# Three steps of each gate's second half summed by TensorE alone, nine reductions there shortened by a second GpSimd addition

## What is computed

```python
def _gate(h, q, Wg, bg, Wq, bq):            # q: 8 x 64 x 768, h: 256 x 768
    h3 = h.reshape(B, N, F)                  # B = 8 blocks of N = 32 nodes
    hg = einsum('bnf,gf->bng', h3, Wg[:, :F])
    qg = einsum('blf,gf->blg', q, Wg[:, F:]) + bg
    attn = sigmoid(hg[:, :, None, :] + qg[:, None, :, :])
    qi = einsum('bnlf,blf->bnf', attn, q)    # sum over the 64 query rows l
    alpha = sigmoid(h3 @ Wq[:, :F].T + qi @ Wq[:, F:].T + bq)
    return alpha * tanh(qi) + (1 - alpha) * h3
```

## Time and profile before

| | us |
|---|---|
| median of 3 runs | 823.54 (823.35 to 824.70) |
| the profiled execution's own time | 824.55 |
| its span in the trace | 822.7 |
| PE busy | 774.9 (94%) |
| DVE busy | 603.2 (73%) |
| POOL busy | 514.3 (63%) |
| ACT busy | 423.7 (52%) |

### The profile page before, as it was taken

How to read it: one execution, slowest core, us unless ns; L and a number is a source line. 1 busy time by engine, 2 the same in 40 slices (tenths; PEclk the granted TensorE clock), 3 DMA queues, 4 the chain that set the end, 5 groups by cost and what they waited for, 6 DMA issues and landing times.

```text
span 822.7 us, 10528 instructions
## 1 busy us (share of the span) xinstructions
PE 774.9 (94%) x4176; PEld 639.7 (78%) x4180; DVE 603.2 (73%) x660; ACT 423.7 (52%) x505; POOL 514.3 (63%) x219
## 2 busy tenths in 40 slices
PE   7999999999988999988898889999999999998998
PEld 4669986776645699667665558999999999975886
DVE  8966239999999631888999997764696498565462
ACT  6424447677664342766676725434442454253731
POOL 0625609999998273599999955770785177805500
PEclk9999999999999999999999999999999999999999
DMA  9037525345332463360153327556356446250001
GB/s 364 31 81 232 170 81 154 89 142 154 115 116 77 137 231 131 77 179 2 52 205 116 115 78 282 180 193 227 116 163 216 159 154 209 99 230 0 2 1 39
DMA packets 24409, 111.01 MB, mean 135 GB/s; under 512 B 3620, under 2 KB 6180, under 8 KB 23976
## 3 DMA queue, kind: packets, MB, share of 16 engines
q1 hardware_dynamic: 23240, 104.24, 39.2%
q10 hardware_dynamic: 1120, 6.10, 1.9%
HBM read 100.63 MB, written 0.79 MB: 123 GB/s over the span
## 4 chain that ended last, share of the span: by engine, by line
PE 57%; POOL 19%; DVE 18%; ACT 3%; issue 2%; DMA 0%; DVEq 0%; ACTq 0%
PE ps L1076 27%; POOL prod L582 13%; DVE prod L1958 10%; PE ps L1107 5%; PE ps L1042 5%; POOL prod L585 4%; DVE qi_t L1976 3%; PE ps L1589 3%; PE ps L1234 2%; PE ps L1255 2%; POOL w_lo L570 2%; PE ps L1413 1%; PE ps L1650 1%; PE ps L1235 1%; PE ps L1304 1%
## 5 line engine op out<-in xcount | busy, mean ns | idle before, releaser
L570 POOL TENSOR_TENSOR w_lo<-w_raw,w_hi 128x1536 fp32r<-128x1536 f32 x49 | 183.9, 3764 | 141.6 <-ACT w_hi L662 141.5
L582 POOL TENSOR_TENSOR prod<-prod 128x1024 f32<-128x1024 f32 x94 | 222.8, 2392 | 46.0 <-DVE prod L1958 45.8
L798 ACT ACTIVATE prod<-ps 128x1024 f32<-128x1024 f32 x192 | 187.3, 1023 | 73.3 <-PE ps L1366 61.0
L1958 DVE TENSOR_TENSOR prod<-prod,ps 128x2048 f32<-128x2048 f32 x96 | 217.8, 2281 | 5.1 <-ACT prod L798 3.4
L662 ACT ACTIVATE w_hi<-w_raw 128x1536 fp32r<-128x1536 f32 x60 | 88.9, 1487 | 119.6 <-PE ps L1076 108.2
L1366 PE MATMUL ps<-sel_pair,h_and_q 128*128 128x512 f32 x384 | 128.4, 447 | 16.8 <-ACT prod L798 16.5
L1076 PE MATMUL ps<-w_hi,yt_hi 128*128 128x384 f32 x480 | 123.0, 337 | 0.2 <-POOL w_lo L570 0.2
L1076 PE MATMUL ps<-w_hi,yt_lo 128*128 128x384 f32 x480 | 122.0, 335 | 0.0
L1076 PE MATMUL ps<-w_lo,yt_hi 128*128 128x384 f32 x480 | 122.0, 335 | 0.0
L1366 PEld LDWEIGHTS ps<-sel_pair,h_and_q 128*128 128x128 f32 x384 | 67.0, 190 | 52.0 <-ACT prod L798 31.8
L1042 PE MATMUL ps<-w_raw,h_t 128*128 128x384 f32 x312 | 106.8, 486 | 0.0
(11 more groups left out here) (247 smaller groups left out, 1093.1 us busy)
## 6 DMA issues: line engine op xcount, KB each, us to landing
w_raw<-weights SPq DMA_DIRECT2D x105, 768.0 KB, 4.4
wa_in<-weights SPq DMA_DIRECT2D x6, 768.0 KB, 5.9
w_gat<-weights SPq DMA_DIRECT2D x6, 768.0 KB, 8.0
w_query<-weights SPq DMA_DIRECT2D x3, 768.0 KB, 11.7
h_and_q<-stage_hi SPq DMA_DIRECT2D x24, 96.0 KB, 2.1
h_and_q<-stage_lo SPq DMA_DIRECT2D x24, 96.0 KB, 2.2
a_vec<-gat_vectors ACTq DMA_DIRECT2D x1, 2048.0 KB, 9.7
q_t<-queries ACTq DMA_DIRECT2D x1, 1536.0 KB, 10.5
```

Of the source, the lines that this page charges most:

```text
L570: pool.tensor_tensor(Wl[:, j, :], raw_slab(U, 0, j), Wh[:, j, :], ALU.subtract).then_inc(w_lo_by_pool, 1)
L582: pool.tensor_tensor(v[:, :, 0:32], v[:, :, 0:32], v[:, :, 32:64], ALU.add).then_inc(folded_once, 1)
L798: act.activation(slot_view(s)[:, :, 32 * u:32 * u + 32], args.rearrange("p b (n l) -> p (b n) l", l=LH), ACT.Sigmoid).then_inc(sigmoid_rea ...
L1958: TT(slot_view(s), slot_view(s), ps[:, 6, o:o + L].unsqueeze(1).broadcast_to([P, NB, L]), ALU.mult).then_inc(products_ready, 1)
```

## The change

In each gate's second half three steps that were "tensor" become "whole": 32, 41 and 43 in gate 0, and 32, 35 and 38 in gate 1. POOL does nothing for a "whole" step, and PE folds all 2048 columns with sixteen identity products instead of eight; both pieces of the sigmoid of step s + 4 then wait for this fold. Nine steps that were "vector" become "pool": 34, 37, 40, 42 and 45 in gate 0, and 34, 40, 42 and 44 in gate 1. Places in the order do not move.

```diff
-ALONE = [(4, 10, 16, 25, 27, 28, 30, 34, 37, 40, 42, 45), (25, 27, 28, 30, 34, 40, 42, 44)]
+ALONE = [(4, 10, 16, 25, 27, 28, 30), (25, 27, 28, 30)]
+WHOLE = [(32, 41, 43), (32, 35, 38)]
 def kind_of(i, s):
+    if s in WHOLE[i]:
+        return "whole"
     if s + 3 in FOLD_AT[i]:
         return "tensor"
     return "vector" if s in ALONE[i] else "pool"
...
+        def by_tensor(i, s):
+            return count_kind(i, s, "tensor") + count_kind(i, s, "whole")
+        def by_pool(i, s):
+            return (STEPS - 1) * i + s + 1 - count_kind(i, s, "whole")
...
             def fold(i, s):
+                if KIND[i][s] == "whole":
+                    return
...
                     if s >= PSLOTS:
-                        if u == 1:
-                            act.wait_ge(folded_once, (STEPS - 1) * i + (s - PSLOTS + 1))
-                        elif KIND[i][s - PSLOTS] == "tensor":
-                            act.wait_ge(fold_ready, count_kind(i, s - PSLOTS, "tensor"))
+                        if u == 1 and KIND[i][s - PSLOTS] != "whole":
+                            act.wait_ge(folded_once, by_pool(i, s - PSLOTS))
+                        elif KIND[i][s - PSLOTS] in ("tensor", "whole"):
+                            act.wait_ge(fold_ready, by_tensor(i, s - PSLOTS))
...
                     bank7_free(at_)
-                    pe.wait_ge(folded_once, (STEPS - 1) * i + (s + 1))
+                    n = 8
+                    if KIND[i][s] == "whole":
+                        pe.wait_ge(products_ready, STEPS * i + (s + 1))
+                        n = 16
+                    else:
+                        pe.wait_ge(folded_once, by_pool(i, s))
...
-                    for k in range(8):
-                        mm = pe.matmul(o, ident[:], slot_view(s)[:, :, 4 * k:4 * k + 4], start=(k == 0), stop=(k == 7))
+                    for k in range(n):
+                        mm = pe.matmul(o, ident[:], slot_view(s)[:, :, 4 * k:4 * k + 4], start=(k == 0), stop=(k == n - 1))
```

More of the change, by code:

```diff
@@ L79 @@
 KIND = [[kind_of(i, s) for s in range(STEPS - 1)] for i in range(2)]
-REST_AT = [[s + (3 if KIND[i][s] == "tensor" and KIND[i][s + 1] != "tensor" else 2) for s in range(STEPS - 1)] for i in range(2)]
+REST_AT = [[s + (3 if s + 3 in FOLD_AT[i] and s + 4 not in FOLD_AT[i] else 2) for s in range(STEPS - 1)] for i in range(2)]
 QUERY_EVENTS = [0, 1, 5, 6]
@@ L583, in fold @@
                 if KIND[i][s] == "pool":
-                    pool.wait_ge(folded_once, (STEPS - 1) * i + (s + 1))
+                    pool.wait_ge(folded_once, by_pool(i, s))
                     pool.tensor_tensor(v[:, :, 0:16], v[:, :, 0:16], v[:, :, 16:32], ALU.add).then_inc(folded_twice, 1)
@@ L1966, in reduce @@
                         terms = slot_view(s)
-                    elif KIND[i][s] == "tensor":
-                        dve.wait_ge(fold_ready, count_kind(i, s, "tensor"))
+                    elif KIND[i][s] in ("tensor", "whole"):
+                        dve.wait_ge(fold_ready, by_tensor(i, s))
                         terms = ps[:, 7, 0:4 * NB].rearrange("p (n l) -> p n l", l=4)
@@ L1973, in reduce @@
                     else:
-                        dve.wait_ge(folded_once, (STEPS - 1) * i + (s + 1))
+                        dve.wait_ge(folded_once, by_pool(i, s))
                         terms = slot_view(s)[:, :, 0:32]
```

## The result

| | us |
|---|---|
| median of the changed kernel, 4 runs | 829.74 (829.16 to 830.85) |
| median of the kernel before, 4 runs | 823.88 (823.35 to 824.70) |
| ratio | 1.0070, 95% interval 1.0055 to 1.0084 |
| span of the profiled execution (before) | 827.4 (822.7) |
| DVE busy (before) | 599.3 (603.2) |

The change makes the kernel slower by 5.9 us (0.7%), with less work on both engines that bound the gates. The forecast was 827.7, so 2.0 us too low; the measured time lies just inside the upper end of its range (829.8). Of the 2.0 us, 0.3 is the median before, which was 823.54 over three runs and is 823.88 over four; 1.7 is the change itself, forecast at +4.2.

A forecast was written before the change was run, and what follows sets the result against it. DVE and POOL were taken to share the bound in the gates' second halves, with the order of waits deciding. Gate 0 +2.4 and gate 1 +1.8 gave +4.2 us, from 823.54 to 827.7; range 825.2 to 829.8 for 8 in 10.

The forecast's parts named there:

- The direction and the mechanism: Both gates' second halves: slower because POOL's chain decides, 827.7 us, own range 826.3 to 829.2; chance 0.78.
- Gate 0, +2.4: Gate 0's second half: POOL's additions delay reduction 40 and product 43; +2.4 us, bounds +1.9 to +3.6.
- step 32 gives nothing: Gate 0: the dropped addition's 2.33 us give nothing, since step 33 waits for DVE's product anyway.
- step 40's first addition: Gate 0, POOL: it starts at 248.36 instead of 245.75, after second additions of 1.25 and 1.36 us.
- the shift shrinks by one shortened reduction: Gate 0, DVE after product 43: the shift falls from +2.97 to +2.45 us, 0.52 less.
- Gate 1, +1.8: Gate 1's second half: the last reduction ends at 487.8 instead of 486.02; +1.8 us, bounds +0.7 to +2.8.
- The lead of dropped additions 35 and 38: Gate 1, POOL: starts step 39 at 457.5 instead of 459.47, a 2.0 us lead, all it keeps of three dropped additions.
- PE's long folds cost nothing: PE: folds of sixteen products, taken as 3.56 us, cost nothing yet but have no slack at gate 0's end.
- PE becomes the bound: Rival: sixteen products hold PE 4 us or more, gate 0 ends at +3.4, gate 1 hides it; 828.7 us; chance 0.08.
- the balance counts: Rival, faster: POOL can use the dropped additions of steps 32, 35 and 38; about 821.7 us; chance 0.06.
- nothing that can be measured: Rival: second additions shrink or reduction 40's wait is halved, gate 1's last pairs hidden; 823.5 to 824.5 us; chance 0.08.
- Behind both gates the chain goes on over PE, and nothing of a DMA is in it, so the shifts stay.: After each gate: its shift carries unchanged to the kernel's end, so the sum is 2.4 + 1.8 = +4.2 us.

The follow-up runs named there:

- step 32 as before: The changed kernel with step 32 of both gates put back to a first addition on GpSimd and a fold of eight: 830.47 us, ratio 1.0069.
- Whole folds alone: The changed kernel without its nine second additions, those steps reduced from 1024 columns as before; the six whole folds stay: 824.54 us, ratio 0.9997.
- whole folds of eight products: The changed kernel with eight products instead of sixteen in each whole fold, leaving out 32 of 64 columns: 829.32 us, ratio 1.0066.
- filler pair: The changed kernel with twelve unread identity products in PE's wait in gate 1, 827.48 us, beside the changed kernel on the same chip, 829.27 us.
- second additions alone: The changed kernel without its six whole folds, those steps keeping first addition and fold of eight; nine second additions stay: 835.28 us, ratio 1.0128.

## Why the prediction was right, and where it was short

- *The direction and the mechanism* held: POOL's queue decides, and the loss in the gates has the size forecast.
- *Gate 0, +2.4*: measured +2.46. The steps held one by one: step 32 gives nothing (the run with step 32 as before), `gate_add` shifts by the second addition of step 34, step 40's first addition 2.62 us later against 2.61, its second delays product 43, and the shift shrinks by one shortened reduction. PE's fold was 3.49 us against the 3.56 taken, and product 47 waited 0.67 us for its sigmoid against about 1.
- *Gate 1, +1.8*: measured +1.72. The lead of dropped additions 35 and 38 was spent by step 43, and the eight pairs ran without a gap up to the last reduction, which started at 488.45, 0.03 us behind POOL's last addition. Product 42 waited 0.64 us for its sigmoid behind fold 38 and stood 0.1 us later than before, against 0.4.
- *PE's long folds cost nothing*: held. Whole folds alone 0.9997, whole folds of eight products 1.0066 against 1.0070.
- *Rivals*: "PE becomes the bound" is out by those two runs; "the balance counts" is out by whole folds alone, where POOL has six additions less and the time stays; "nothing that can be measured" is out by the ratio, 1.0055 at least.
- *What was short*: the step "Behind both gates the chain goes on over PE, and nothing of a DMA is in it, so the shifts stay." They grow there. The sum lacked a term for PE's clock: PE's wait ahead of the sixth transpose grew from 1.23 us to 3.27, the clock granted behind it fell to half, and 1.3 to 1.5 us were lost in the products that follow (+1.49 and +1.29 in the two profiles of the changed kernel; +1.55 between the two kernels of the filler pair). With it the sum is 4.2 + 1.4 = 5.6, against 5.9 and 5.1 in the two measurements. The forecast itself moved the last reduction from 486.02 to 487.8, and so lengthened PE's wait ahead of the transpose; it was not asked what the engine does after it.
- *How firm that is*: the loss in the gates stands in every profile; the clock's part is less firm, as not every execution falls. Of the second five runs of the changed kernel two had a granted clock of 1.000 and took 827.52 and 827.74 us; the three at 0.996 took 829.27 to 830.60. Two filler runs at 1.000 took 826.77 and 826.96. The kernel before took 822.27 to 823.06 in its six runs at 1.000. So where no execution shows a half clock, the changed kernel still loses some 5.0 us, the gates' 4.2 and 0.8 more, and its filler version 4.2. That difference of 0.8 us nothing here explains, and none of these executions was profiled. The half clock is shown to cost 1.3 to 1.5 us in the executions that have it behind gate 1; that it makes up the whole gap between 4.2 and the medians is not shown, since the kernel before loses time to such stretches as well.

## What to carry to other kernels

When two engines share a bound, add up no balance of their work. Walk along the queue that is the chain, and count removed work only where that engine had no idle time behind it and added work in full where it had none: here 14 us removed from GpSimd gave nothing, and 12 us put on it cost 10.6, some of it perhaps by the clock. Put the relief ahead of the load: the same two means, fewer of each and in that order, made the kernel faster (order and number were not tried apart). And where a change lengthens an idle time of TensorE ahead of work on the chain, look at the granted clock behind it before calling the shift final.

## What the hardware showed

- After 3.27 to 3.31 us without a product on TensorE ahead of the sixth transpose, the granted clock fell to half (1.2 GHz) near its return, in all four profiles with that wait: from 489.6, 489.4, 487.2 and 492.6 us, which is 0.3 us before the transpose to 1.2 behind it. It did so too in the 3.46 us wait of the run with second additions alone. With waits of 0.65 to 1.66 us ahead of the transpose it did not fall there, in eight profiles. It does not take so long a wait everywhere: it fell at 375.7 us already in the kernel before, where PE's waits just ahead were 0.65, 0.18 and 0.60 us. The Trainium skill's page TensorE: Matmul & The Clock Gate, section "HAM oscillation — how this bites in real kernels", tells of a kernel whose products run at half clock behind each wait for data; the traces agree, with a wait for another engine.
- Over executions of one kernel such falls come and go: the kernel before had granted clocks from 0.991 to 1.000, with 822.27 us at 1.000 and 826.85 at 0.991. Part of the spread of the medians is this.
- An identity product of 128 columns in float32 costs 3.49 / 16 = 0.218 us back to back, whether eight or sixteen stand in a row (1.78 / 8 = 0.222 from the earlier trace rows).
